# A 3x3 convolution kernel: six product pairs for five, every second one late in the run, with the sums and offsets moved between VectorE and ScalarE

## The reference

```python
def _gn(v, G=32, eps=1e-05):
    g = v.reshape(B_, G, C_ // G, H_, W_)
    m = jnp.mean(g, axis=(2, 3, 4), keepdims=True)
    s = jnp.var(g, axis=(2, 3, 4), keepdims=True)
    return ((g - m) / jnp.sqrt(s + eps)).reshape(v.shape)
...
x = x + _L0_conv_ref(_gn(x), L0_conv_W)   # conv with sign(W), padding 1
```

## Time and profile before

| what | value |
|---|---|
| median of 3 runs | 205.72 us (204.9 to 205.97) |
| profiled execution, its own time | 205.18 us |
| its span, first to last instruction | 203.3 us |
| PE, DVE, ACT, POOL busy | 190.7, 165.5, 150.3, 166.7 us |
| mean granted TensorE clock | 0.996 of full speed |
| first and last convolution matmul start | 11.41 and 198.5 us |

### The profile page before, as it was taken

The page is one execution under the profiler, slowest core; times in us unless marked ns, Lnnn a source line. Parts: engine busy times, 40 slices in busy tenths (PEclk is TensorE's granted clock), DMA queues, the critical chain, the costliest instruction groups (busy, mean ns, idle before and its releaser), DMA issues.

```text
span 203.3 us, 9960 instructions
## 1 busy us (share of the span) xinstructions
PE 190.7 (94%) x4470; PEld 175.0 (86%) x4470; DVE 165.5 (81%) x363; ACT 150.3 (74%) x143; POOL 166.7 (82%) x85
## 2 busy tenths in 40 slices
PE   1798999999999998999999999999999999999990
PEld 0497978989899997889999979999999998997890
DVE  2999999976999995789999777998878999717392
ACT  3197998798989099598918989790998999596000
POOL 1029987999999999869899997979999799999500
PEclk9999999999999999999999999999999999999998
DMA  6999839819894999956499996469898400924295
GB/s 221 365 403 401 280 110 316 306 45 283 321 339 160 320 412 327 317 202 196 167 326 364 316 375 207 160 217 378 330 340 307 164 3 3 373 108 161 94 350 194
DMA packets 18697, 52.16 MB, mean 257 GB/s; under 512 B 2080, under 2 KB 5024, under 8 KB 18656
## 3 DMA queue, kind: packets, MB, share of 16 engines
q1 hardware_dynamic: 18656, 51.54, 70.8%
HBM read 25.84 MB, written 25.69 MB: 253 GB/s over the span
## 4 chain that ended last, share of the span: by engine, by line
PE 89%; DVE 3%; DMA 3%; issue 2%; SPq 1%; ACT 0%; DVEq 0%
PE psum L716 88%; DMA w_raw<-in_L_conv_W_dram 3%; DVE xbuf L564 1%; DVE xbuf L554 1%; SPq L235 1%; PE psum L630 1%; DVE xbuf L528 1%; PE psum L643 0%; DVE xbuf L540 0%; ACT w_sign L388 0%; DVEq L150 0%
## 5 line engine op out<-in xcount | busy, mean ns | idle before, releaser
L716 PE MATMUL psum<-halves,w_taps 64*64 64x385 f16 (+9 forms) x4140 | 184.6, 325 | 2.3 <-issue 2.3
L716 PEld LDWEIGHTS psum<-halves,w_taps 64*64 64x64 f16 x4140 | 165.5, 107 | 14.0 <-issue 4.3
L312 POOL TENSOR_TENSOR halves<-xnorm,halves 128x784 f16<-128x784 f32 (+5 forms) x35 | 91.5, 2632 | 21.4 <-ACT xnorm L397 21.1
L483 DVE BATCH_NORM_STATS2 stats<-xbuf 128x6 f32<-128x448 f32 x112 | 60.7, 612 | 3.0 <-DMA xbuf<-in_x_dram 2.9
L405 ACT ACTIVATE halves<-xbuf,coef 128x784 f16<-128x784 f32 (+6 forms) x36 | 51.5, 1430 | 3.8 <-DVE coef L508 3.6
L397 ACT ACTIVATE xnorm<-xbuf,coef 128x784 f32<-128x784 f32 (+5 forms) x35 | 50.5, 1442 | 0.0
L418 ACT ACTIVATE moved<-psum 64x784 f32<-64x784 f32 (+1 forms) x30 | 25.5, 849 | 10.9 <-PE psum L716 10.4
L327 POOL TENSOR_TENSOR xbuf<-xbuf,moved 128x784 f32<-128x784 f32 (+1 forms) x15 | 29.2, 1947 | 1.5 <-ACT moved L418 1.5
L540 DVE SCALAR_TENSOR_TENSOR xbuf<-psum,xbuf 128x784 f32<-128x784 f32 x21 | 20.3, 968 | 10.8 <-PE psum L716 10.8
L554 DVE SCALAR_TENSOR_TENSOR xbuf<-psum,xbuf 64x784 f32<-64x784 f32 (+1 forms) x32 | 28.2, 881 | 1.0
L716 PE MATMUL psum<-line_halves,w_products 64*64 64x504 f16 (+1 forms) x180 | 21.6, 373 | 0.2 <-issue 0.2
(11 more groups left out here) (36 smaller groups left out, 68.0 us busy)
## 6 DMA issues: line engine op xcount, KB each, us to landing
xbuf<-in_x_dram SPq DMA_DIRECT2D x48, 448.0 KB, 6.0
out_dram<-xbuf SPq DMA_DIRECT2D x43, 392.0 KB, 3.9
xbuf<-in_x_dram SPq DMA_DIRECT2D x16, 224.0 KB, 5.9
out_dram<-xbuf SPq DMA_DIRECT2D x5, 504.0 KB, 5.7
out_dram<-xbuf SPq DMA_DIRECT2D x5, 448.0 KB, 2.7
out_dram<-xbuf SPq DMA_DIRECT2D x5, 364.0 KB, 3.5
out_dram<-xbuf SPq DMA_DIRECT2D x5, 252.0 KB, 4.8
out_dram<-xbuf SPq DMA_DIRECT2D x1, 224.0 KB, 2.7
```

The costliest lines, as they stand in the source:

```text
L312: nc.gpsimd.tensor_tensor(at(halves[:, k % HRING, 1, :], a, b), at(xnorm[:, k % NRING, :], a, b), at(halves[:, k % HRING, 0, :], a, b), AL ...
L483: nc.vector.bn_stats(stats[:, n, :], xbuf[:, s, n * STAT:(n + 1) * STAT]).then_inc(blocks_ready, 1)
L716: mm = pe.matmul(outs[:, :, left:right], weights, ins[:, :, left + dx:right + dx], start=first_step, stop=last_step)
```

## The change

One more pair goes by products, and from pair 8 every second pair does. A plain pair between two product pairs (4, 9, 11, 13) leaves PSUM by VectorE alone: it takes over away unit 1, which ScalarE moved and GpSimd added; it does so before the statistics. From pair 2 on ScalarE makes the negated mean, the scaled variance and the offsets. VectorE makes the whole of pair 0's first chunk, and ScalarE copies the weights first. The warm-up has 17 rounds in front of the signs and 4 behind the transposes. In pair 0 the upper halves of the first two blocks of each kind come before their lower halves.

```diff
-WARM_UP = 11
-KEEP_WARM = 7
+WARM_UP = 17
+KEEP_WARM = 4
-WINOGRAD = (3, 6, 9, 12, 14)
+WINOGRAD = (3, 5, 8, 10, 12, 14)
     def by_scalar(k, i):
-        return k != LAST and i == (0 if k in WINOGRAD else 1)
+        if k in WINOGRAD:
+            return i == 0
+        return k != LAST and i == 1 and not (k - 1 in WINOGRAD and k + 1 in WINOGRAD)
...
# GpSimd and ScalarE: the guard of add_away(k - 2, 1) and of move_away(k - 2, 1)
-                if k >= 2 and k - 2 not in WINOGRAD:
+                if k >= 2 and by_scalar(k - 2, 1):
...
# ScalarE
             def deviation(k):
                 act.wait_ge(var_ready, k + 1)
                 nc.scalar.activation(std[:], own[:, 1:2], ACT.Sqrt, bias=eps[:], scale=QUARTER).then_inc(std_ready, 1)
+                if k >= 2:
+                    nc.scalar.mul(minus_mean[:], own[:, 0:1], -1.0)
+                    nc.scalar.activation(var[:], own[:, 1:2], ACT.Identity, bias=eps[:], scale=QUARTER).then_inc(var_scaled, 1)
+
+            def offsets(k):
+                s = k % XRING
+                act.wait_ge(coef_ready, k + 1)
+                act.wait_ge(var_scaled, k - 1)
+                nc.scalar.activation(coef[:, s, 1:2], minus_mean[:], ACT.Identity, scale=coef[:, s, 0:1]).then_inc(offset_ready, 1)
+                act.wait_ge(offset_ready, k + 1)
+                if k in WINOGRAD:
+                    nc.scalar.mul(coef[:, s, 2:3], coef[:, s, 1:2], 2.0).then_inc(twice_ready, 1)
...
             act.wait_ge(w_turned, 1)
-            w_copy(0)
+            for n in range(KH):
+                w_copy(n)
             for k in range(NP):
...
-                act.wait_ge(coef_ready, 3 * (k + 1))
+                if k >= 2:
+                    offsets(k)
+                else:
+                    act.wait_ge(offset_ready, k + 1)
...
                 for c in range(len(chunks(k))):
-                    hi(k, c)
-                    if (k, c) == (0, 0):
-                        w_copy(1)
-                        w_copy(2)
-                    else:
+                    if (k, c) != (0, 0):
+                        hi(k, c)
                         normalise(k, c)
...
# VectorE: aggregate and scale
-                dve.wait_ge(var_ready, k + 1)
-                nc.vector.tensor_scalar(var[:], own[:, 1:2], QUARTER, EPS * QUARTER,
-                                        ALU.mult, ALU.add).then_inc(coef_step, 1)
+                if k < 2:
+                    dve.wait_ge(var_ready, k + 1)
+                    nc.vector.tensor_scalar(var[:], own[:, 1:2], QUARTER, EPS * QUARTER,
+                                            ALU.mult, ALU.add).then_inc(coef_step, 1)
...
+                if k >= 2:
+                    dve.wait_ge(var_scaled, k - 1)
...
-                dve.wait_ge(coef_ready, 3 * k + 1)
-                nc.vector.tensor_scalar(coef[:, s, 1:2], own[:, 0:1], -1.0, coef[:, s, 0:1],
-                                        ALU.mult, ALU.mult).then_inc(coef_ready, 1)
-                nc.vector.tensor_scalar(coef[:, s, 2:3], own[:, 0:1], -2.0, coef[:, s, 0:1],
-                                        ALU.mult, ALU.mult).then_inc(coef_ready, 1)
+                if k < 2:
+                    dve.wait_ge(coef_ready, k + 1)
+                    nc.vector.tensor_scalar(coef[:, s, 1:2], own[:, 0:1], -1.0, coef[:, s, 0:1],
+                                            ALU.mult, ALU.mult).then_inc(offset_ready, 1)
             def early_chunk():
                 a, b = chunks(0)[0]
-                dve.wait_ge(coef_ready, 2)
-                nc.vector.tensor_scalar(at(halves[:, 0, 0, :], SHARED, b), at(xbuf[:, 0, :], SHARED, b),
+                dve.wait_ge(offset_ready, 1)
+                nc.vector.tensor_scalar(at(halves[:, 0, 0, :], a, b), at(xbuf[:, 0, :], a, b),
...
                 if k - 1 in WINOGRAD:
                     add_outer(k - 1)
+                if k >= 1 and not by_scalar(k - 1, 1):
                     add_away(k - 1, 1)
                 if 1 <= k < NP - 2:
                     pair_stats(k + 2, range(NSTAT))
...
# TensorE's order in pair 0
+                if k == 0:
+                    for half in range(2):
+                        for here, there in zip(home[:2], away[:2]):
+                            for n in range(half * TAPS, (half + 1) * TAPS):
+                                step(here, n)
+                                step(there, n)
+                    h = a = 2
                 while h < len(home) or a < len(away):
```

More of the change, by code:

```diff
@@ L141, in chunks_before, with chunks_by @@
         return sum(len(chunks(i)) for i in range(k))
-    SHARED = 8
+    def chunks_by(k, c):
+        return chunks_before(k) + c
     PIECES = [(0, 16), (16, 32), (32, 48), (48, 56)]
@@ L175, in conv_preact_kernel @@
         own = sb("own", [128, 2], F32)
+        minus_mean = sb("minus_mean", [128, 1], F32)
         var, std, inv, dev, eps, warm = [sb(name, [128, 1], F32)
@@ L195, in conv_preact_kernel @@
         coef_ready = sem("coef_ready")
+        offset_ready = sem("offset_ready")
+        twice_ready = sem("twice_ready")
+        var_scaled = sem("var_scaled")
         xnorm_early = sem("xnorm_early")
@@ L309, in lo @@
                 a, b = chunks(k)[c]
-                pool.wait_ge(xnorm_ready, chunks_before(k) + c)
-                pool.wait_ge(hi_ready, chunks_before(k) + c + 1)
+                pool.wait_ge(xnorm_ready, chunks_by(k, c))
+                pool.wait_ge(hi_ready, chunks_by(k, c))
                 nc.gpsimd.tensor_tensor(at(halves[:, k % HRING, 1, :], a, b), at(xnorm[:, k % NRING, :], a, b),
@@ L379, in _ @@
                     add_away(k - 1, 0)
-            if LAST - 1 not in WINOGRAD:
+            if by_scalar(LAST - 1, 1):
                 add_away(LAST - 1, 1)
@@ L401, in hi @@
                 a, b = chunks(k)[c]
-                if (k, c) == (0, 0):
-                    b = SHARED
                 s = k % XRING
@@ L434, in line_upper @@
                 act.wait_ge(lines_made, 3 * n + 3)
+                act.wait_ge(twice_ready, n + 1)
                 nc.scalar.activation(line_halves[:, 0, SUM], lines[:, SUM], ACT.Identity,
@@ L483, in pair_stats, with steps_before @@
                     nc.vector.bn_stats(stats[:, n, :], xbuf[:, s, n * STAT:(n + 1) * STAT]).then_inc(blocks_ready, 1)
+            def steps_before(k):
+                return 4 * k - max(0, k - 2)
             def aggregate(k):
@@ L665, in wait_upper @@
                 if b.product is None:
-                    pe.wait_ge(hi_ready, chunks_before(k) + last_chunk(b) + 1)
                     if (k, last_chunk(b)) == (0, 0):
                         pe.wait_ge(hi_early, 1)
+                    else:
+                        pe.wait_ge(hi_ready, chunks_by(k, last_chunk(b)))
                 else:
@@ L679, in wait_lower @@
                 else:
-                    pe.wait_ge(lo_ready, chunks_before(k) + last_chunk(b))
+                    pe.wait_ge(lo_ready, chunks_by(k, last_chunk(b)))
             def step(b, n):
```

8 lines of the change are left out of this document (3 added, 5 removed).

## The result

The changed kernel took 209.31 us (median of 4 runs, 209.08 to 209.53) against 205.84 us of the kernel before beside it (4 runs, 204.9 to 209.38): ratio 1.0145 [1.0104, 1.0186]. The forecast was 205.4 us with a range up to 206.9. The profiled execution took 209.1 us, its span 207.3.

What follows compares the result with a forecast made beforehand. TensorE's convolution line, 88% of the span, bounds the kernel. -1.31 - 0.24 + 0.1 + 1.75 - 0.1 = +0.2 us, less 0.4 hidden by gaps, is -0.2: forecast 205.4 us, range 203.9 to 206.9.

Steps and rivals of the forecast that it cites:

- The gaps: TensorE's gaps of the "issue" kind, 2.5 us in 187, would hide 0.4 us of the added waits.
- GpSimd step: At pair 5, GpSimd's lower halves are ready at 72.6, just when TensorE asks: no margin, +0.1 us.
- rival 2: SyncE's loads come late behind GpSimd's sums; VectorE's statistics wait in steps 5, 8 or 10: 206.5 to 208 us; chance 0.18.
- VectorE's waits: Ends of pairs 5, 10 and 12: TensorE waits for VectorE's added away units, 0.55 + 0.55 + 0.65 = +1.75 us.
- Rival 1: The waits on VectorE stay hidden and time follows TensorE's columns: 203.7, against the median 204.3 us; chance 0.30.
- ScalarE: Offsets moved to ScalarE: 0.9 to 1.2 us more a pair, load covered; pair 13's scale 0 to 0.3 us late.
- The start: VectorE makes the whole first chunk from 10.40; first convolution matmul at 11.17 in place of 11.41: -0.24 us.
- rival 3: The start's 0.24 us is lost at pair 5 because GpSimd's clock doesn't move with it; counted inside the forecast.
- The sixth pair: One more plain pair becomes a product pair: 11.82 - 10.51 = -1.31 us of TensorE.

Runs made afterwards that it cites:

- thin stores: The changed kernel with stores of pairs 2 to 12 writing one row each, most output left out: 204.28 us, ratio 0.9862.
- loads first: The changed kernel, SyncE issuing a product pair's last two load pieces ahead of the store that waits for GpSimd: 204.77 us, ratio 0.9885.
- old list: The changed kernel with product pairs 3, 6, 9, 12, 14 as before: 207.1 us, ratio 1.0033.
- new list alone: The kernel before with only the product pairs changed, to 3, 5, 8, 10, 12, 14: 207.98 us, ratio 1.004.
- pairs between by ScalarE: The changed kernel with product pairs' loads ahead of the store, and pairs 4, 9, 11, 13 leaving PSUM by ScalarE and GpSimd as before: 207.2 us, ratio 1.0045.
- the other list: The changed kernel with product pairs' loads ahead of the store, and product pairs 4, 6, 8, 10, 12, 14: 203.97 us, ratio 0.9855.
- all loads first: The kernel before with a load's two pieces ahead of the store in every half step of SyncE's queue: 202.91 us, ratio 0.9874.

## Why the prediction was wrong, by its own steps

**The gaps (failed).** The step was "Off this goes what gaps of the 'issue' kind hide: 2.5 us in 187 ... I take 0.4". It took the gaps for a stock that stays where it is and only covers other waits. They come and go with the kernel's own traffic. (Term by term in the two profiled executions the GpSimd step below is missed by more, 2.8 us for 0.1; but thin stores and loads first keep that wait and are still faster than the kernel before.) The change cost gaps in pairs 6 to 15, from 0.8 to 4.6 us, where the list is dense and the lines of one product pair come ahead of the sum of the last. Fewer bytes took them to nothing (204.28), another order of the queue took most of them (204.77), GpSimd's sum put first took 2.8 us off from the other side (206.53), all against 209.31. The kernel before gains by the new order too (202.91), so the gaps aren't the whole difference: TensorE ends 3.7 us later after than before, and 1.7 us later (197.66 against 195.97) where neither has a gap behind pair 0 (one execution each). Some 2.0 of the 3.7 us go with the gaps, the rest with the engines' waits below.

**The held queue (rival 2, right place, wrong victim).** The rival saw that the sums come late behind the lines and that SyncE's queue waits for them, though its 44.2 us were plain pairs' waits and the product pairs' were 39.0. Its price, VectorE's statistics waiting for loads in steps 5, 8 and 10, didn't come (their 3.3 us of waits for loads stand at the start, and the loads took 7.1 us to land in place of 6.0). TensorE's instructions paid, which no rival had. Over the runs that store everything the link shows: where the queue waited for GpSimd 83 us or more in all (before, after, old list, new list alone, pairs between by ScalarE), TensorE's listed gaps are 2.3 to 3.9 us; where it waited 78 or less, 0 to 0.6, but for the profiled execution of the other list, the longest of its four (66.2 and 3.0). The total doesn't tell before (83.2, 2.5) from after (83.6, 3.9); why after has more stays open.

**GpSimd (mis-sized).** The step was "no margin, and I take +0.1 us". Measured: 1.6 us in pair 3, which it didn't look at, and 1.15 in pair 5. GpSimd's rows at pair 3 to 5:

```profile
62.20 1.27 POOL L346 TENSOR_TENSOR lines<-xbuf 128x504 f32<-128x504 f32 x1
...
66.92 2.12 POOL L335 TENSOR_TENSOR xbuf<-xbuf,moved 128x896 f32<-128x896 f32 x1
68.99 4.60 POOL L320 TENSOR_TENSOR halves<-xnorm,halves 128x1456 f16<-128x1456 f32 x2
```

The working's chain is right to the hundredth: 4.72 + 2.07 + 4.60 behind its anchor give the 73.59 at which TensorE's halves were ready. The anchor was wrong: 62.20, not the 61.20 that the kernel before had the earlier trace rows. Pair 3 shows how: its lower halves came 1.0 us later (50.02 against 49.03) while TensorE came 1.5 us earlier (pair 2 ended at 47.21 against 48.72). It asks for them some 1.1 us behind that end, so 0.8 us to spare became 1.7 us of lateness. The lateness is partly ScalarE's small operations, here ahead of pair 2's upper halves. Before and after:

```profile
26.14 0.29 ACT L392 ACTIVATE std<-own,eps 128x1 f32<-128x1 f32 x1
28.15 1.74 ACT L405 ACTIVATE halves<-xbuf,coef 128x1624 f16<-128x1624 f32 x1
```
```profile
26.56 0.29 ACT L400 ACTIVATE std<-own,eps 128x1 f32<-128x1 f32 x1
26.76 0.19 ACT L402 ACTIVATE minus_mean<-own 128x1 f32<-128x1 f32 x1
26.85 0.28 ACT L403 ACTIVATE var<-own,eps 128x1 f32<-128x1 f32 x1
...
28.84 0.29 ACT L410 ACTIVATE coef<-minus_mean,coef 128x1 f32<-128x1 f32 x1
29.17 1.74 ACT L424 ACTIVATE halves<-xbuf,coef 128x1624 f16<-128x1624 f32 x1
```

From the square root to the upper halves it is 2.61 us in place of 2.01: 0.6 of the 1.0. The other 0.4 was there ahead of it, 26.56 against 26.14. The new start counts too: alone it gives a wait of 0.9 in pair 3, there because TensorE comes earlier. A part of the 2.8 us took the place of early gaps, 1.9 in pairs 3 and 5, which would have covered it.

**VectorE's waits (mechanism right, size near, covered here).** Forecast 0.55 to 0.65 at the ends of pairs 5, 10 and 12. Without gaps 0.50 and 0.50 showed at 10 and 12; at 5 GpSimd's lateness took its place, as the working allowed. In the change itself the gaps covered all but 0.15 in 13. (Pair 12 is 0.42 over the ruler, but most of it is at 165.28, inside the pair, behind a late packet.) Rival 1, that they stay hidden, was right on the waits and wrong on the time: what hid them, gaps, cost more than they.

**ScalarE (not foreseen).** Its load was rightly called covered and the latency of the scale watched. The wait that came is another: the square root and two new operations (0.58 us together) stand ahead of its move out of PSUM at the end of pair 8, done at 119.96, and TensorE resumed at 120.00, 0.4 to 0.6 late.

**The start (−0.24; the chunk sized right, but late, and the gain lost).** VectorE's chunk took 0.72 against 0.71 foreseen, but began at 10.73, not 10.40, because its statistics waited for the first load:

```profile
6.92 1.68 DVE L504 BATCH_NORM_STATS2 stats<-xbuf 128x6 f32<-128x448 f32 x3 [0.57 <-DMA xbuf<-in_x_dram]
...
10.73 0.72 DVE L542 TENSOR_SCALAR halves<-xbuf,coef 128x840 f16<-128x840 f32 x1
```

So the first convolution matmul came at 11.50, not 11.17 (before: 11.41); pair 0 ended 0.15 earlier beside the gap that it lost. GpSimd took it back at pair 3, two pairs before the place that rival 3 named.

**The sixth pair (−1.31, right).** The rulers held: product pairs 8 and 14 took 10.53 and 10.51.

**Left without gaps.** Pairs 1 to 15 take 173.97 us in the run with thin stores and 170.89 in the kernel before with all loads first, both with no gap there: the change is then 3.1 us worse (−1.3, +2.8 GpSimd, +1.6 ScalarE and VectorE), of which its earlier pair 0 gives back 1.4, part of that the other run's later weights and gap. The measured ratios, 0.9862 [0.9794, 0.9931] and 0.9874 [0.9806, 0.9941], are too wide to show this difference.

## What to carry to other kernels

A gap with no releaser need not be chance: look at what the DMA moved in the 10 us before it, and put loads ahead of a store that waits for a late engine, since one in-order queue turns an engine's lateness into a burst. When an engine is credited with an earlier arrival, recompute the anchor of every chain that feeds it, for a margin of 0.8 us is gone when one side gains 1.5 and the other loses 1.0. Price an added wait both with and without the gaps that cover it today.

## What was unexpected of the hardware

A gap in TensorE's stream cost up to 1.6 us of a pair, and nine of nine ended 2.2 to 2.5 us behind the start of a 16 KB instruction packet, which itself takes 1 us whether a gap follows or not. The Trainium skill ("Runtime: NRT & Kernel Launch", Instruction fetch mechanics) calls the crossing of such a block mostly hidden; in the kernel before with all loads first it was, from pair 1 on, and in the changed kernel the gaps behind such packets cost 4.6 us. What exactly delays the packet stays open: pair 10 of the reordered kernel ran with the DMA at 0.89 and had no gap, and the gap at 148.71 came when the burst had ended. The kernel before also scattered more than its first three runs showed, 203.92 to 208.88 over 25 runs in one group, so that 0.5% was too fine a measure of no change (the intervals here are 0.4 to 0.7% either way), while its reordered version stayed within 202.2 to 203.74 in four.
